# Fp32 products with the identity become TensorE transposes, in eight stages of a one-core kernel

## The reference

```python
x = x + L0(_gn(x))      # attention with a position bias: 4 heads, 4096 keys, softmax
x = x + L1(_gn(x))      # projection, depthwise conv, selective scan in 4 directions, norm, gate, projection
t = tokens(x)
t = t + L2_attn(_ln_t(t))   # softmax attention, 1 head of 128, 4096 keys
t = t + L2_ffn(_ln_t(t))    # spectral convolution over the tokens
t = t + L3_attn(_ln_t(t))   # linear attention
t = t + L3_ffn(_ln_t(t))    # 8 experts, the best two by token
```

## Time and profile before

| | before |
|---|---|
| median of 3 runs | 8602.94 us (8586.87 to 8607.12) |
| profiled execution | 8596.49 us, its span 8594.5 us |
| PE busy | 7730.8 us, 90% of the span, 42744 matmul records |
| VectorE (DVE), ScalarE (ACT), GpSimd (POOL) busy | 6553.7, 4582.8, 6072.9 us |
| granted PE clock, mean over the span | 0.94 |

### The profile page before, as it was taken

The page is one execution under the profiler, slowest core; times in us unless marked ns, Lnnn a source line. Parts: engine busy times, 40 slices in busy tenths (PEclk is TensorE's granted clock), DMA queues, the critical chain, the costliest instruction groups (busy, mean ns, idle before and its releaser), DMA issues. The chain is left out here.

```text
span 8594.5 us, 127535 instructions
## 1 busy us (share of the span) xinstructions
PE 7730.8 (90%) x42744; PEld 5606.9 (65%) x42744; DVE 6553.7 (76%) x7404; ACT 4582.8 (53%) x12756; POOL 6072.9 (71%) x3149
## 2 busy tenths in 40 slices
PE   6999999999996759999999999778999988888798
PEld 3444444444442358888888888646868778888775
DVE  5677677676664669999999999756867639999634
ACT  3544544545442467777777777424656515545304
POOL 1767767767771479999999999604868709999505
PEclk7999999999997769999999999888989999988898
DMA  6222222222213564444444444441000110000000
GB/s 172 45 58 51 56 51 48 59 45 56 46 32 128 196 222 104 109 106 104 107 108 108 106 106 110 161 172 56 23 18 23 43 39 8 1 1 1 21 9 21
DMA packets 517251, 628.76 MB, mean 73 GB/s; under 512 B 284104, under 2 KB 320464, under 8 KB 508816
## 3 DMA queue, kind: packets, MB, share of 16 engines
q1 hardware_dynamic: 516624, 620.94, 26.6%
HBM read 413.32 MB, written 173.81 MB: 68 GB/s over the span
## 5 line engine op out<-in xcount | busy, mean ns | idle before, releaser
L1684 POOL TENSOR_TENSOR m_c_h<-m_h,m_c 128x2048 f32<-128x2048 f32 x520 | 2341.3, 4563 | 45.9 <-DVE m_h L1671 45.8
L1671 DVE TENSOR_TENSOR_SCAN m_h<-m_decay,m_ps_x 128x1024 f32<-128x1024 f32 x1040 | 2271.3, 2262 | 91.5 <-issue 64.4
L1584 PE MATMUL m_ps_y<-m_c_h,m_ident 128*128 128x256 f32 x8320 | 1978.0, 381 | 2.1 <-POOL m_c_h L1684 2.1
L1002 DVE TENSOR_REDUCE l_max_by_cell<-l_ps_all 128x32 f32<-128x512 f32 x2048 | 1321.6, 685 | 700.5 <-PE l_ps_all L792 693.9
L930 ACT ACTIVATE l_probs<-l_ps_all 128x512 f32<-128x512 f32 x2048 | 1077.2, 602 | 1219.0 <-PE l_ps_all L828 1218.2
L1584 PEld LDWEIGHTS m_ps_y<-m_c_h,m_ident 128*128 128x128 f32 x8320 | 1509.8, 190 | 174.5 <-POOL m_c_h L1684 4.2
L987 POOL TENSOR_TENSOR l_probs_added<-l_probs 128x512 f32<-128x512 f32 x704 | 902.8, 1282 | 663.6 <-ACT l_probs L930 659.4
L2698 POOL TENSOR_TENSOR s_late<-s_late,s_products 128x1024 f32<-128x1024 f32 x352 | 857.9, 2479 | 306.4 <-ACT s_products L2680 306.3
L2238 POOL TENSOR_TENSOR l_probs_low<-l_probs,l_probs_high 128x512 fp32r<-128x512 f32 x512 | 663.7, 1302 | 577.2 <-ACT l_probs_high L2221 562.5
L1608 ACT ACTIVATE m_b_diagonals<-m_steps,m_b_rows 128x32 fp32r<-128x32 f32 x4160 | 966.9, 306 | 3.1 <-DMA m_b_rows<-b_t 3.0
L2649 PE MATMUL s_ps_all<-s_m_parts,s_bins_high 128*128 128x256 f32 x4096 | 805.3, 298 | 155.3 <-DVE s_acc L2739 149.4
(11 more groups left out here) (390 smaller groups left out, 11898.5 us busy)
## 6 DMA issues: line engine op xcount, KB each, us to landing
m_delta_u<-du_t SPq DMA_DIRECT2D x1040, 128.0 KB, 3.6
m_c<-c_windows SPq DMA_DIRECT2D x130, 512.0 KB, 4.2
l_queries<-q_parts SPq DMA_DIRECT2D x192, 256.0 KB, 4.7
du_t<-m_delta_u_high SPq DMA_DIRECT2D x128, 256.0 KB, 3.0
du_t<-m_delta_u_low SPq DMA_DIRECT2D x128, 256.0 KB, 3.0
ys<-m_y SPq DMA_DIRECT2D x256, 126.0 KB, 4.8
m_direction<-ys SPq DMA_DIRECT2D x12, 2048.0 KB, 13.8
l_q_parts<-q_parts SPq DMA_DIRECT2D x32, 512.0 KB, 8.2
```

Of the source, the lines that this page charges most:

```text
L1002: dve.tensor_reduce(dst, src, AX.X, ALU.max).then_inc(max_taken, 1)
L1584: ins = pe.matmul(y_ps[:, group % 2, 0:DIRS * SPAN].rearrange("p (d t) -> p d t", d=DIRS), ident[:, :], ch[:, group % CH, :, n, :], start= ...
L1671: dve.tensor_tensor_scan(h[:, u % H, :], decay[:, pair % 2, ct, k % 2, :, :].rearrange("p n t -> p (n t)"), x_ps[:, u % X, :], 0.0, ALU.mu ...
L1684: pool.tensor_tensor(ch[:, group % CH, 2 * pair % DIRS:2 * pair % DIRS + 2, :, :].rearrange("p d n t -> p d (n t)"), h[:, 2 * pair % H:2 * ...
```

## The change

The nine sites call `pe.transpose` in place of `pe.matmul` with the same operands. In `turn` of `bias_attention` the column is broadcast to 128 columns instead of 64 and the result is written to all 128 partitions of its bank; VectorE still reads 64. No wait, no order and no other instruction changes. The diff, with the three sites that read like the first left out:

```diff
@@ layer_norm (the same in layer_norm_kept, mamba_finish and norm_kept)
-  ins = pe.matmul(wide_ps[:, t % 2, n * P:(n + 1) * P], rstd[:, q, col:col + 1].to_broadcast((P, P)), ident[:, :], start=True, stop=True)
+  ins = pe.transpose(wide_ps[:, t % 2, n * P:(n + 1) * P], rstd[:, q, col:col + 1].to_broadcast((P, P)), ident[:, :])
@@ bias_attention, turn
-  ins = pe.matmul(ps[0:SIDE, TURNED, k * P:(k + 1) * P], mx[:, k:k + 1].to_broadcast((P, SIDE)), ident[:, :], start=True, stop=True)
+  ins = pe.transpose(ps[:, TURNED, k * P:(k + 1) * P], mx[:, k:k + 1].to_broadcast((P, P)), ident[:, :])
@@ full_attention, turn
-  ins = pe.matmul(ps[:, MAX0, k * P:(k + 1) * P], mx[:, k:k + 1].to_broadcast((P, P)), ident[:, :], start=True, stop=True)
+  ins = pe.transpose(ps[:, MAX0, k * P:(k + 1) * P], mx[:, k:k + 1].to_broadcast((P, P)), ident[:, :])
@@ full_attention, spread_inverse
-  ins = pe.matmul(ps[:, MAX0 + 1, k * P:(k + 1) * P], inv[:, k:k + 1].to_broadcast((P, P)), ident[:, :], start=True, stop=True)
+  ins = pe.transpose(ps[:, MAX0 + 1, k * P:(k + 1) * P], inv[:, k:k + 1].to_broadcast((P, P)), ident[:, :])
@@ spectral_back
-  ins = pe.matmul(ps[:, n % 8, q * P:(q + 1) * P], mid[:, :, :, :, 4 * (n - TURN) + q], ident[:, :], start=True, stop=True)
+  ins = pe.transpose(ps[:, n % 8, q * P:(q + 1) * P], mid[:, :, :, :, 4 * (n - TURN) + q], ident[:, :])
@@ experts
-  ins = pe.matmul(gt_ps[:, c * P:(c + 1) * P], gates[:, c * P:(c + 1) * P], ident[:, :], start=True, stop=True)
+  ins = pe.transpose(gt_ps[:, c * P:(c + 1) * P], gates[:, c * P:(c + 1) * P], ident[:, :])
```

More of the change, by code:

```diff
@@ L1806, in spread_out @@
                     col = k * (TW // P) + j
-                    ins = pe.matmul(wide_ps[:, n % 2, j * P:(j + 1) * P], rstd[:, q, col:col + 1].to_broadcast((P, P)), ident[:, :], start=True, stop=True)
+                    ins = pe.transpose(wide_ps[:, n % 2, j * P:(j + 1) * P], rstd[:, q, col:col + 1].to_broadcast((P, P)), ident[:, :])
                 ins.then_inc(spread, 1)
```

## The result

The changed kernel takes 8535.22 us (median of 4 runs, 8525.73 to 8546.92) against 8598.95 us for the kernel before in all its 4 runs: a ratio of 0.9928, 95% interval 0.991 to 0.9945, so 64 us or 0.7% faster. The forecast was 8510, its range 8478 to 8555. The profiled execution of the changed kernel took 8525.73 us, its span 8523.7, which is 70.8 less than the span before.

The account below looks back on a forecast made before the run. PE was taken to bound the stages holding most of the products. Gains of 13.6 - 5 + 32 + 12 + 35 + 4 + 0.9 = 92.5 us, taken from 8602.9, gave 8510 us, range 8478 to 8555.

Parts of the forecast that it names:

- What one transpose costs: All sites: a transpose is one record instead of two, so four take 0.44 us instead of 0.98 at high clock.
- full attention: Its turns and spreads: each takes 0.44 us instead of 0.81, 12 us gained, bounds 6 and 14.
- Spectral back: Its blocks at L2797: half the records, 35 us gained, bounds 28 and 42.
- The warm norms: s_ln and ln4, at the high clock: 6.8 us gained in each, 13.6 together.
- The cold norms: ln2 and ln5, at the low clock: clock rises later, 5 us lost together, bounds 14 gained and 25 lost.
- the two terms: The norms' forecasts: 13.6 us gained in s_ln and ln4, 5 us lost in ln2 and ln5.
- The first rival: ln2 and ln5: clock stays low throughout, 25 us lost instead of 5, total 8530 us; chance 0.28.
- The second rival: Norms and spectral back: transposes do not raise the clock at all, total 8537 us; chance 0.06.
- mamba_finish: Its spreads: VectorE sets the pace, so only some count, 4 us gained, bounds 1 and 8.6.
- Bias attention: The turn shortens by 0.57 us a row and the row-bias chain moves along: 32 us gained, bounds 7 and 36.
- the third rival: Bias attention: row-bias copies don't move, waits at L828 grow and the clock falls, total 8638 us; chance 0.03.

Follow-up runs that it names:

- e7: Kernel before with only the spreads of the norms ln2, s_ln, ln4 and ln5 as transposes: 8581.92 us, ratio 0.9972.
- e8: Kernel before with only full attention's turns and spreads and spectral back's blocks as transposes: 8567.41 us, ratio 0.9956.
- e3: Changed kernel, SyncE reordered in bias attention: inverses sent, high copies, inverses' spread, low copies, table load last: 8497.88 us, ratio 0.9883.
- e4: Changed kernel with added identity transposes ahead of and between the means of the four norms: 8534.37 us, ratio 0.9922.
- e1: Kernel before with only the turn of bias attention as a transpose: 8627.86 us, ratio 1.0026.
- e2: Kernel before, turn still a product, with the SyncE order of e3: 8601.73 us, ratio 0.9995.
- e9: Changed kernel with only SyncE's table load moved behind the row-bias copies in bias attention: 8485.47 us, ratio 0.9875.
- e10: Changed kernel with both the table load and the spread of the inverses behind all row-bias copies: 8454.03 us, ratio 0.9841.
- e12: As e9, but with the turn of bias attention as the product of before: 8513.38 us, ratio 0.9908.
- e11: As e10, but with the turn of bias attention as the product of before: 8493.1 us, ratio 0.9884.

## Why the prediction was right in its number and wrong in one term

**What one transpose costs** held: 0.47 us for the four in ln4 where 0.44 was forecast, 0.35 in full attention, so that stage gained 16.9 us for 12 (14.7 by 32 times 0.46; the stages of e7 and e8 differ by 12.9).

**Spectral back** held: 18.8 us between the bounds of 14.2 and 28.2, 37.7 gained where 35 was taken.

**The warm norms** held: 6.8 us a norm forecast, 5.9 to 7.2 measured at like clock.

**The cold norms** failed in the safe direction. "5 us lost" rested on ln2 and ln5 being the cold ones and staying cold for longer. Which norm is cold, and for how long, is not a property of the norm: in the changed kernel's own profile ln4 was low for 27.3 us and in e3 for 6.8. The four gained some 24 us together (e7, interval 15 to 34) where the two terms gave 8.6. The first rival, a clock that stays low through ln2 and ln5, did not come: in the changed kernel's profile ln2 was low for 13.5 of its 51.2 us (34.2 of 68.3 before) and ln5 for 20.5 of 49.5 (17.1 of 54.3 before).

**The clock in transposes alone.** The second rival, that transposes don't raise the clock, is out: L2797 ran at 1.00 with nothing else on PE, and with the transposes added in e4 the four norms were low for 24.9 us, where the other profiles with transposes in the norms have 52 to 96. The rule of the Trainium skill behind it ("TensorE: Matmul & The Clock Gate", "Part 4: PE-mode transpose"), that the clock doesn't engage for transposes, isn't what these traces show.

**mamba_finish** can't be told: 4.1 us in the first pair, but over the profiles the stage took 247.4 to 251.5 with products (before, e1, e2, e7, e8) and 244.1 to 250.2 with transposes (the nine others).

**Bias attention is the step that failed:** "So the rounding, and the copies and the wait at L828 behind it, move with PE. Some of it is lost where SyncE is still busy with the inverses. I take 0.5 x 64 = 32 us", with 7 as the lower bound. The stage lost 6 us instead. The rounding did move, by 0.49. The copies did not. These are means over rows 2 to 61, in us from the first record of the turn: the end of the rounding, the start of the high copies, from the end of the last copy's issue to the next L828, and the distance to the next turn; then the rows in which the clock dropped. 28 of them have a table load, 32 have not.

| | rounding ends | copies start | issue to L828 | to next turn | rows with a drop |
|---|---|---|---|---|---|
| before, 28 with a load | 3.17 | 3.61 | 1.91 | 38.70 | 3 |
| after, 28 with a load | 2.68 | 3.64 | 1.95 | 39.23 | 13 |
| e9, 28 with a load | 2.68 | 3.13 | 1.50 | 37.63 | 1 |
| e10, 28 with a load | 2.68 | 2.75 | 1.45 | 37.31 | 0 |
| before, 32 without | 3.23 | 3.57 | 1.47 | 37.83 | 2 |
| after, 32 without | 2.80 | 3.36 | 1.45 | 37.64 | 3 |
| e10, 32 without | 2.82 | 2.91 | 1.48 | 37.29 | 2 |

Without a load the turn gained 0.19 us a row, for SyncE comes from the inverses at 3.25 (end of L718) and can't start the copies at 2.80. With a load it lost 0.53: the copies start no earlier, PE's wait grows by what the turn gave, and ten more rows lose the clock behind it, which at 1.5 us each is the 15 us of 28 x 0.53. 28 x 0.53 - 32 x 0.19 = 8.8 us lost, the stage's 6 to 9. That is the third rival, in 28 rows instead of 64; it was given 3 in 100 because the argument against it looked only at the rounding. The prediction named its sign, growing waits at L828, and by that sign this term was wrong. The trace of before held the answer: in the row shown above SyncE is through at 851.36 and the rounding at 851.38, and in the 32 rows without a load L718 ends at 3.27 on average and the rounding at 3.23. Two chains end together, so that shortening one alone can gain little or nothing.

e9 to e12 settle the cause. With the table load behind the copies, both the start (3.64 to 3.13) and the time to L828 (1.95 to 1.50) fall and the drops go; with the inverses' spread behind them too, the copies start 0.07 behind the rounding. There the turn is worth 28 us of the stage (e11 to e10), and 31 in the order of e3, so 32 was about its price once nothing else ends at the same time. In e9, where the inverses still stand ahead of the copies in every row, it is 19. The time to L828 is a matter of the landing: in the changed kernel a high copy lands 4.3 us after its issue and a low one 2.9 (means over the 28 rows with a load), against 2.3 and 2.0 in the 32 others, and 2.3 and 2.0 in the 28 rows of e9, where the load comes behind them. This delay does not come from the turn (before: 4.2 and 2.8), and so moving the load gains with the product too (e12).

**The sum.** 92.5 us forecast, 70.8 in the pair of profiled executions: 38 missing in bias attention, 6 better in the norms, 8 in full attention and spectral back, 3 in stages that the change doesn't touch. The time fell into the range because its slow end stood 45 us above the forecast, which leaves room for one miss of 38, and because the norms and the two large blocks gave 14 us more than forecast. That the norms did so was not foreseen, so the number owes a part to luck.

## What to carry to other kernels

Where a shortened step feeds a copy or transfer, find everything that the transfer's start waits for, the order of the issuing queue included: if two chains end together (here 0.02 us apart in the row shown), shortening one gains little or nothing until the other is moved. A wait that grows on TensorE costs more than its length when the clock falls behind it. And what an issuing queue has ahead of an urgent transfer is an order that can be changed at no cost: here one load moved behind the copies gained 46 to 50 us, against the 64 of the whole change, and 11 to 19 us in the kernel whose turn was still a product.

## What was not expected of the hardware

A wait of 1.86 us was followed by a drop of the clock that cost 1.5 us more. Small copies of 32 KB landed 4.3 us after their issue instead of 2.3 when 512 KB had been asked for just ahead of them. Four transfers issued by ScalarE cost it 2.44 us, as on SyncE (2.41), but in the path of everything behind them. A stage that runs the same instructions took 57.4 or 68.3 us (ln2) in different executions, by when its clock rose.
